# Transposing node rows in 128-column chunks that cross row boundaries, with five skip weight blocks

## The reference

```
h  = relu(layernorm(x))                       # per node row
s, v = h[:, :64], h[:, 64:]                   # 64 scalars, 32 vectors
skip_s = s @ W_skip0                          # 64 -> 96
skip_v = einsum('nmi,mk->nki', v, W_skip1)    # 32 -> 32, for each component i
w   = relu(edge_feature @ W_fc1) @ W_fc2      # edges: products of w, h[dst] and directions
agg = segment_sum(products, src) / 32
out_s = agg_s @ W_out_s + skip_s
out_v = einsum(agg_v, W_out_v) + skip_v
fs   = silu(out_s[:, :64]);  gate = sigmoid(out_s[:, 64:96])
out  = x + concat(fs, gate * out_v)
```

## Time and profile before

| | |
|---|---|
| median of the timed runs | 1324.63 us |
| span of the profiled execution | 1322.7 us |
| TensorE matmul busy | 1197.9 us (91%) |
| VectorE busy | 1099.5 us (83%) |
| ScalarE busy | 1029.0 us (78%) |
| GpSimd busy | 828.6 us (63%) |
| HBM traffic over the span | 160 GB/s |

### The profile page before, as it was taken

The page is one execution under the profiler, slowest core; times in us unless marked ns, Lnnn a source line. Parts: engine busy times, 40 slices in busy tenths (PEclk is TensorE's granted clock), DMA queues, the critical chain, the costliest instruction groups (busy, mean ns, idle before and its releaser), DMA issues.

```text
span 1322.7 us, 33310 instructions
## 1 busy us (share of the span) xinstructions
PE 1197.9 (91%) x8853; PEld 998.1 (75%) x8853; DVE 1099.5 (83%) x4058; ACT 1029.0 (78%) x2446; POOL 828.6 (63%) x1077
## 2 busy tenths in 40 slices
PE   4899998999999999994999998999889999889986
PEld 2455557888888888883888787888778888778876
DVE  7999998888889888875688788888788888788775
ACT  2777776788878888864888788888888887888884
POOL 5555557787878888712766566566566666566651
PEclk9999997999999999996999999999999999999998
DMA  6000002344434443422888878888878888888873
GB/s 214 8 0 0 0 15 65 105 111 111 112 104 113 112 110 108 113 60 52 218 248 245 251 225 246 248 248 253 238 231 241 253 245 248 239 235 255 241 192 108
DMA packets 90930, 212.40 MB, mean 161 GB/s; under 512 B 15030, under 2 KB 56281, under 8 KB 90878
## 3 DMA queue, kind: packets, MB, share of 16 engines
q1 hardware_dynamic: 62462, 155.23, 35.4%
q0 software_dynamic: 28416, 56.56, 21.0%
HBM read 127.73 MB, written 84.00 MB: 160 GB/s over the span
## 4 chain that ended last, share of the span: by engine, by line
PE 38%; DVE 18%; ACT 9%; issue 9%; DMA 8%; POOL 2%; SPq 0%; DVEq 0%; ACTq 0%; POOLq 0%
DMA xb<-x 7%; PE bank L1419 6%; PE bank L1349 5%; DVE n_stat L858 5%; ACT nn L1178 4%; DVE ob L949 4%; PE bank L1289 4%; PE bank L1378 3%; PE bank L1366 3%; PE bank L1433 3%; PE bank L1362 3%; PE bank L1364 3%; PE bank L1334 2%; PE bank L1411 2%; DVE ob L956 2%
## 5 line engine op out<-in xcount | busy, mean ns | idle before, releaser
L574 POOL DMA_INDIRECT mg<-messages,slot_m x392 | 430.0, 1097 | 274.5 <-issue 107.3
L1178 ACT ACTIVATE nn<-xb,n_bias,n_rstd 128x160 f32<-128x160 f32 x784 | 383.7, 650 | 91.0 <-DVE n_bias L656 91.0
L1419 PE MATMUL bank<-wsk_a,nt 128*128 128x160 f32 x1568 | 298.8, 313 | 58.3 <-DVE ob L949 57.0
L1419 PEld LDWEIGHTS bank<-wsk_a,nt 128*128 128x128 f32 x1568 | 227.2, 192 | 75.7 <-issue 57.2
L501 POOL DMA_INDIRECT xg<-x,dst_g x200 | 208.8, 1044 | 61.4 <-issue 56.1
L858 DVE BATCH_NORM_STATS2 n_stat<-xb 128x6 f32<-128x160 f32 x784 | 203.0, 314 | 29.1 <-DMA xb<-x 28.4
L949 DVE SCALAR_TENSOR_TENSOR ob<-sg,bank 128x128 f32<-128x128 f32 x588 | 131.7, 281 | 100.8 <-ACT ob L1193 100.7
L1433 PE MATMUL bank<-mg,hot 64*128 64x192 f32 x1568 | 181.8, 351 | 4.7 <-DVE hot L934 4.7
L1411 PE MATMUL bank<-ident,nn 128*128 128x128 f32 x784 | 147.8, 312 | 13.7 <-ACT nn L1178 13.7
L1185 ACT ACTIVATE nt<-bank 128x640 f32<-128x640 f32 x196 | 137.5, 702 | 23.2 <-PE bank L1412 18.5
L1411 PEld LDWEIGHTS bank<-ident,nn 128*128 128x128 f32 x784 | 110.1, 209 | 58.1 <-issue 57.4
(11 more groups left out here) (187 smaller groups left out, 2476.2 us busy)
## 6 DMA issues: line engine op xcount, KB each, us to landing
xb<-x SPq DMA_DIRECT2D x97, 640.0 KB, 6.9
out_dram<-ob SPq DMA_DIRECT2D x97, 640.0 KB, 3.6
messages<-msg SPq DMA_DIRECT2D x50, 390.6 KB
mg<-messages,slot_m POOLq DMA_INDIRECT x392
ef<-edge_feat_t SPq DMA_DIRECT2D x50, 125.0 KB, 5.9
xg<-x,dst_g POOLq DMA_INDIRECT x200
xb<-x SPq DMA_DIRECT2D x1, 420.0 KB
out_dram<-ob SPq DMA_DIRECT2D x1, 420.0 KB
```

Source lines behind the costliest of these rows:

```text
L574: pool.indirect_dma_start(mg[:, m, k, :], None, messages[:, :], bass.IndirectOffsetOnAxis(ap=slot_m[:, m, k:k + 1], axis=0)).then_inc(n.g[ ...
L1178: last = act.activation(nn[:, u % 2, h, :, g % 4], xb[:, u, g, :], ACT.Relu, bias=n_bias[:, u // U, c:c + 1], scale=n_rstd[:, u // U, c:c ...
L1419: pe.matmul(z[:, t, 0:F], nt[:, h, t * P:(t + 1) * P], wsk_a[:], start=(t % 2 == 0), stop=False, skip_group_check=True)
```

## The change

Each half's `nn` becomes 4 x 160 numbers side by side (640), the four rows one after the other. TensorE transposes five chunks of 128 columns, whatever row they fall in: chunk 0 is row 0 up to its column 127; chunk 1 the last 32 of row 0 and 96 of row 1; chunk 2 the last 64 of row 1 and the 64 scalars of row 2; chunk 3 the last 96 of row 2 and the first 32 of row 3; chunk 4 the rest of row 3. Each chunk has a weight block of its own in `wsk` (128 x 800): 160, 160, 96, 192 and 192 columns. Block 2 is split by rows: partitions 0 to 63 give 64 columns of row 1, partitions 64 to 127 give 96 columns of row 2, each a matmul of its own into its own PSUM bank. In PSUM, z lies as 4 x 192 across the bank boundary, so every product writes one stretch.

The diff, cut to its core:

```
-        wsk_a = sb("wsk_a", [P, SG + 2 * V])
-        wsk_z = sb("wsk_z", [P, 4 * V])
+        SKIP = (0, F, 2 * F, 2 * F + SG, 2 * F + SG + Z, 2 * F + SG + 2 * Z)
+        wsk = sb("wsk", [P, SKIP[5]])
-        nn = sb("nn", [P, 2, 2, F, 4])
+        nn = sb("nn", [P, 2, 2, 4 * F])
...
-            weight_loads += [(wsk_z[j:P:4, cols], w_skip1), (wnl_z[j:P:4, cols], w_nl1)]
+            weight_loads.append((wnl_z[j:P:4, cols], w_nl1))
+        for c, row, col in ((0, 0, 0), (1, V, V), (2, S, 0)):
+            weight_loads.append((wsk[row:row + S, SKIP[c] + col:SKIP[c] + col + SG], w_skip0))
+        weight_loads += [(wsk[P - V:P, SKIP[3] + 3 * V:SKIP[3] + 3 * V + SG], w_skip0[0:V, :]),
+                         (wsk[0:V, SKIP[4]:SKIP[4] + SG], w_skip0[V:S, :])]
+        for c, row, col in (...12 places...):
+            weight_loads.append((wsk[row:row + V, SKIP[c] + col:SKIP[c] + col + V], w_skip1))
...
-            q_z = [bank[2 + h][:, :].rearrange("p (t c) -> p t c", c=TS) for h in range(2)]
+            q_z = [bank[2 + h][:, 512 - 2 * Z:512 + 2 * Z].rearrange("p (t c) -> p t c", c=Z) for h in range(2)]
...
-                dve.tensor_scalar(wsk_a[:, SG:F], wsk_a[:, SG:F], 0.5, None, ALU.mult)
-                last = dve.tensor_scalar(wsk_z[:], wsk_z[:], 0.5, None, ALU.mult)
+                for first, cols in ((SKIP[0] + SG, 2 * V), (SKIP[1], V), (SKIP[1] + V + SG, V), (SKIP[3], 3 * V),
+                                    (SKIP[4] + SG, 3 * V)):
+                    dve.tensor_scalar(wsk[:, first:first + cols], wsk[:, first:first + cols], 0.5, None, ALU.mult)
+                last = dve.tensor_scalar(wsk[0:S, SKIP[2]:SKIP[2] + S], wsk[0:S, SKIP[2]:SKIP[2] + S], 0.5, None, ALU.mult)
...
-                            last = act.activation(nn[:, u % 2, h, :, g % 4], xb[:, u, g, :], ACT.Relu,
+                            last = act.activation(nn[:, u % 2, h, g % 4 * F:g % 4 * F + F], xb[:, u, g, :], ACT.Relu,
...
-                        for t in range(4):
-                            pe.transpose(q_t[h][:, t * P:(t + 1) * P], nn[:, u % 2, h, 0:P, t], ident[:])
-                        pe.transpose(q_t[h][:, 4 * P:5 * P], nn[:, u % 2, h, P:F, :], ident[:]).then_inc(n.t, 1)
+                        for c in range(5):
+                            last = pe.transpose(q_t[h][:, c * P:(c + 1) * P], nn[:, u % 2, h, c * P:(c + 1) * P], ident[:])
+                        last.then_inc(n.t, 1)
...
-                        for t in range(4):
-                            pe.matmul(z[:, t, 0:F], nt[:, h, t * P:(t + 1) * P], wsk_a[:], start=(t % 2 == 0),
-                                      stop=False, skip_group_check=True)
-                            if t % 2 == 1:
-                                j = t // 2
-                                pe.matmul(z[:, 2 * j:2 * j + 2, F:Z], nt[:, h, 4 * P:5 * P],
-                                          wsk_z[:, 2 * V * j:2 * V * j + 2 * V],
-                                          start=False, stop=every, skip_group_check=True)
+                        for c, first in ((0, 512 - 2 * Z), (1, 512 - 2 * Z + F), (3, 512 + SG), (4, 512 + Z)):
+                            cols = SKIP[c + 1] - SKIP[c]
+                            pe.matmul(z[:, first:first + cols], nt[:, h, c * P:(c + 1) * P], wsk[:, SKIP[c]:SKIP[c + 1]],
+                                      start=(c % 3 == 0), stop=every, skip_group_check=True)
+                        for part, first, cols in ((slice(0, S), 512 - 2 * V, 2 * V), (slice(S, P), 512, SG)):
+                            pe.matmul(z[:, first:first + cols], nt[part, h, 2 * P:3 * P], wsk[part, SKIP[2]:SKIP[2] + cols],
+                                      start=False, stop=every, skip_group_check=True)
```

More of the change, by code:

```diff
@@ L299, in gnn_layer @@
                          (wo_u[0:2 * V, 0:V], w_out_v[S:S + 2 * V, :]),
-                         (wsk_a[0:S, 0:SG], w_skip0), (wnl_a[0:S, 0:S], w_nl0)]
+                         (wnl_a[0:S, 0:S], w_nl0)]
         for j in range(2):
@@ L303, in gnn_layer @@
             rows = slice(S + V * j, S + V * j + V)
-            weight_loads += [(wsk_a[rows, SG + V * j:SG + V * j + V], w_skip1),
-                             (wnl_a[rows, S + V * j:S + V * j + V], w_nl1)]
+            weight_loads.append((wnl_a[rows, S + V * j:S + V * j + V], w_nl1))
         for j in range(4):
             cols = slice(V * j, V * j + V)
-            weight_loads += [(wsk_z[j:P:4, cols], w_skip1), (wnl_z[j:P:4, cols], w_nl1)]
+            weight_loads.append((wnl_z[j:P:4, cols], w_nl1))
[3 more added lines that the diff above has]
+                         (wsk[0:V, SKIP[4]:SKIP[4] + SG], w_skip0[V:S, :])]
+        for c, row, col in ((0, S, SG), (0, S + V, SG + V), (1, 0, 0), (1, V + S, V + SG), (2, 0, 0), (2, V, V),
+                            (3, 0, 0), (3, V, V), (3, 2 * V, 2 * V),
+                            (4, V, SG), (4, 2 * V, SG + V), (4, 3 * V, SG + 2 * V)):
+            weight_loads.append((wsk[row:row + V, SKIP[c] + col:SKIP[c] + col + V], w_skip1))
         def wait(eng, s, value):
@@ L606, in link @@
                     dve.wait_ge(s_dve_steps, steps[0])
-                for t in (wfc1, wo_v, wo_u, wsk_a, wsk_z, wnl_a, wnl_z, row0, zeros_w):
+                for t in (wfc1, wo_v, wo_u, wsk, wnl_a, wnl_z, row0, zeros_w):
                     last = dve.memset(t[:], 0.0)
@@ L1409, in turn @@
                         wait(pe, n.ht, 2 * i + h - 1)
-                        for t in range(4):
-                            pe.transpose(q_t[h][:, t * P:(t + 1) * P], nn[:, u % 2, h, 0:P, t], ident[:])
-                        pe.transpose(q_t[h][:, 4 * P:5 * P], nn[:, u % 2, h, P:F, :], ident[:]).then_inc(n.t, 1)
+                        for c in range(5):
+                            last = pe.transpose(q_t[h][:, c * P:(c + 1) * P], nn[:, u % 2, h, c * P:(c + 1) * P], ident[:])
+                        last.then_inc(n.t, 1)
                     def skip(i, h):
-                        z = q_z[h]
+                        z = bank[2 + h]
                         pe.wait_ge(n.ht, 2 * i + h + 1)
                         wait(pe, n.mul, 2 * i + h - 1)
-                        for t in range(4):
-                            pe.matmul(z[:, t, 0:F], nt[:, h, t * P:(t + 1) * P], wsk_a[:], start=(t % 2 == 0),
-                                      stop=False, skip_group_check=True)
-                            if t % 2 == 1:
-                                j = t // 2
-                                pe.matmul(z[:, 2 * j:2 * j + 2, F:Z], nt[:, h, 4 * P:5 * P],
-                                          wsk_z[:, 2 * V * j:2 * V * j + 2 * V],
-                                          start=False, stop=every, skip_group_check=True)
+                        for c, first in ((0, 512 - 2 * Z), (1, 512 - 2 * Z + F), (3, 512 + SG), (4, 512 + Z)):
[5 more added lines that the diff above has]
+                                      start=False, stop=every, skip_group_check=True)
                     def add(i, u, h):
```

## The result

| | before | after |
|---|---|---|
| median of 12 timed runs each, one chip | 1324.93 us | 1318.25 us |
| ratio of the runs | | 0.9944 (95% interval 0.9924 to 0.9964) |
| span of the profiled execution | 1322.7 us | 1317.1 us |
| VectorE's waits for x | 28.4 us, 36 times | 34.7 us, 47 times |

The change is faster by 0.56%, 6.7 us. Forecast were 1319.8 us and a gain of 4.8.

The account below looks back on a forecast made before the run. Node-stage rounds were bound by VectorE, ScalarE or TensorE, with DMA close behind. -3.6 - 1.4 + 0.24 = -4.8 us from 1322.7 gave 1317.9, plus 1.9 around the span: 1319.8 us; own range 1316 to 1323, 8-in-10 range 1306 to 1327.

Parts of the forecast that it names:

- the 22 periods: Node stage, repeats of four rounds: 0.27 us saved each, 0.16 after DMA, 3.6 us in all.
- the last rounds: Last 8 rounds, where no x is loaded: they keep all of TensorE's saving, 8 x 0.18 = 1.4 us.
- What bounds the rounds: Node stage, four rounds between residuals: VectorE sets the 9.25 us one, ScalarE the 5.63, TensorE the 6.30 and 6.82.
- the long round: Node stage, every fourth round, which works out the scales: set by VectorE's chain to `n_bias`, 9.25 us, forecast to stay.
- the short round: Node stage, round that catches up piled-up work: set by ScalarE without a pause, 5.63 us, forecast to stay at 5.6.
- TensorE's half, -0.09: TensorE, node stage: per half, skip products save 0.05 us and transposes 0.04, so 6.24 a macro becomes 6.06.
- The split block pairs: Skip products' row-split block: its four narrow passes run as two side-by-side pairs, 0.22 us a half.
- the rival with 1335.5 us: Split block's narrow passes run one after another, 0.44 us for 0.22; +10.9 us; chance 0.12.
- ScalarE: the stride costs 0.13 of the duration but only 0.01 of the step: ScalarE's normalisation: side-by-side writing shortens it to about 520 ns, but the next start hardly moves; gain counted as nothing.
- the first rival: ScalarE's next normalisation starts 0.13 us earlier, saving 17 us beside the 4.8: 1303 us; chance 0.14.
- DMA takes 0.4 of the gain: Node stage: loads of x land only partly earlier, VectorE waits more; 0.6 kept, 0.16 of 0.27 us a period.
- Off the node stage, +0.24: Before the node stage: ten more weight DMAs cost nothing, four more VectorE scalings add 0.24 us.

Follow-up runs that it names:

- half stores: Each macro's output store writes only its first four of eight row groups: 1318.03 us on the kernel before, 1308.56 us on the changed kernel.
- the load first: SyncE issues the load of x ahead of the output store, all bytes kept: changed kernel 1307.33 us, kernel before 1318.05 us.
- TensorE alone: Changed kernel with ScalarE writing rows interleaved again, 16 bytes apart: 1326.59 us, ratio 0.9999 to the kernel before; with half stores 1309.91 us.
- ScalarE alone: Kernel before with only ScalarE writing the four normalised rows side by side: 1323.23 us, ratio 0.9976; with half stores 1315.28 us.

## Why the prediction was right, point by point

- *The sum.* In the two profiled executions, the 22 periods took 3.9 us less (forecast 3.6), the last rounds 1.2 less (forecast 1.4), and the rest 0.5 less (forecast 0.24 more). The range was added up a little short: 22 x 0.35 + 2 below 1324.6 is 1315, not 1316.
- *What bounds the rounds.* Right where x lands in time, and only in part in the changed kernel as it stands. With half stores or the load first, the long round stands near 9.2 whatever TensorE does. TensorE alone makes the third round 0.17 shorter and the fourth 0.28, and with the load first the whole change makes the fourth 0.30 shorter, for 0.16 a half. But the forecast had the short round keep its work, and its residuals 5.6, 6.2 and 6.65 apart; they came 5.42, 6.29 and 6.88. ScalarE takes 0.20 off the short round, and of that and TensorE's saving together the sum of short and third keeps 0.19. In the fourth the waits for x take most of the saving.
- *TensorE's half, -0.09.* Direction right, size -0.16. Nearly all of the difference is in the transposes: -0.09, not -0.04, since the first one's step fell as well. Skip products and messages together were right, -0.06 for -0.05, in other shares: full-height passes took 1.29 to the first narrow one, where 1.21 + 0.09 was put, the four narrow passes 0.27, not 0.22, and the messages 0.80, not 0.86.
- *The split block pairs.* Right, and shown by undoing it: the rival with 1335.5 us was the price of not pairing, and the unsplit block pays 0.20 a half.
- *ScalarE: the stride costs 0.13 of the duration but only 0.01 of the step.* The duration came as forecast (515 for 520). The step fell by 0.026, not 0.01: the forecast had added 0.03 for 32 more numbers to a 0.40 step that probably held a wait of its own; that is not shown. The size counts, for the forecast then put ScalarE at nothing, and eight steps of 0.026 make up the short round's 0.20. How little of it reaches the end by itself is seen in ScalarE alone, with a third round of 6.42. In the first rival the step fell by 0.13; it fell by 0.026: the line rule of the Trainium skill's page SBUF — State Buffer bears on the duration here, and hardly on the step.
- *DMA takes 0.4 of the gain.* The weakest step. That DMA closes off gains is right, and the waits for x grew from 28.4 to 34.7 us as written. But the reason given, that at 265 GB/s a macro needs 6.4 us, failed: at the same bytes and the load first the waits fall to 4.8 us. And the share was a guess: TensorE's saving alone lost all, both together lost 3 of 9.5 us or 4 of 10.7.
- *Off the node stage, +0.24.* Too small to see: the first residual came at 630.8 us in place of 631.5, and over the other runs anywhere from 629.7 to 632.4.

So the number came near (4.8 for 6.7) in part by luck: a half that was undersized and a ScalarE step that was left out met a loss to DMA whose share nobody had measured.

## What to carry to other kernels

Two transfers that wait for the same event should be issued in the order in which somebody needs them: here the order of two lines was worth 0.9%, more than the 0.56% of the change, and it hid part of what the change was worth. Before pricing a saving in a stage that also streams, take the wait for the stream away in an experiment, by fewer bytes or another order, and read the rounds, not the sum. Read neighbouring rounds together, since one can give back what the other saved. In this kernel a matmul split by rows paid next to other 64-partition work, and cost where it stood alone.

## What the runs showed of the hardware

- An activation that writes fp32 numbers 16 bytes apart lasted 650 ns, 8 bytes apart 526, side by side 515 (160 numbers, two per-partition operands); the next one started 0.437, 0.413 and 0.411 us later. Most of the stride's price is overlapped.
- Four passes over 64 partitions, two on the lower and two on the upper half, took 0.27 us ahead of others of their kind, 0.39 ahead of full-height ones, and 0.51 as full-height passes, the step to 64-partition passes included. That step costs 0.09: the last full-height pass of 192 columns takes 0.256 in place of 0.162.
- Five transposes with 128-number operands read side by side took 0.601 us to the next product, 0.694 where four of them read 16 bytes apart; 0.057 of the 0.093 is in the first step.
- With a load of 640 KB issued ahead of the store of 640 KB that it had stood behind, and so 0.54 us sooner, the waits for loads fell from 34.7 to 4.8 us, while DMA moved 250 in place of 247 GB/s.
